# Third convolution tile's taps ahead of the split of the sums, and the residual added to h by VectorE late in the turn, in the state space stage of a four-stage language model kernel

## What is computed

```python
def _block(x, ...):                          # x: layernorm(h)
    h = _ln(x, ln1_w, ln1_b)
    zxbcdt = einsum('bld,pd->blp', h, in_proj_w)     # z | xBC | dt
    xBC = silu(sum(xp[:, k:k+L] * conv_w[:, k] for k in range(4)) + conv_b)
    dt = softplus(dt + dt_bias); dA = exp(dt * -exp(A_log))
    # recurrence over 512 steps: hn = hprev*dA + dt*x (outer) B ; y = hn . C
    y = (ys + D_skip * xs) * silu(z)
    y = y * rsqrt(mean(y*y) + EPS) * ssm_norm_w
    x = x + einsum('bli,di->bld', y, out_proj_w)     # called x2 in the kernel
    f = einsum('bld,hd->blh', _ln(x, ln2_w, ln2_b), fc1_w)
    f = f[..., :HIDDEN] * silu(f[..., HIDDEN:])
    return x + einsum('blh,dh->bld', f, fc2_w)
h = h + _block(_layernorm(h), ...)
```

## Time and profile before

| what | value |
|---|---|
| median of 3 runs | 2181.28 us (2177.38 to 2182.77) |
| the profiled execution | 2185.66 us |
| its span in the profile | 2183.2 us |
| state space stage | about 930 to 1398 us of the span |
| from the end of one turn to the end of the next, middle turns | 51.0 us |
| TensorE busy | 1947.5 us (89%) |
| VectorE busy | 1153.1 us (53%) |
| ScalarE busy | 743.0 us (34%) |
| GpSimd busy | 443.9 us (20%) |

### The profile page before, as it was taken

One profiled execution on the slowest core, in us unless ns is written; L12 is line 12 of the kernel. 1 busy time (PEld: TensorE's weight loads), 2 busy tenths in 40 slices (PEclk: granted clock), 3 DMA queues, 4 the chain that ended last, 5 costly groups with the idle time before them and its releaser, 6 DMA issues. The chain is left out here.

```text
span 2183.2 us, 27922 instructions
## 1 busy us (share of the span) xinstructions
PE 1947.5 (89%) x10040; PEld 1224.6 (56%) x10048; DVE 1153.1 (53%) x2695; ACT 743.0 (34%) x1249; POOL 443.9 (20%) x534
## 2 busy tenths in 40 slices
PE   4997618999999999758999998699999999999997
PEld 2343503344444444435556655465567888888886
DVE  5798577666666665246777776337412222222221
ACT  1434002554555545444555554121111111111111
POOL 5200200120122111111211111110371322322232
PEclk9988558999999999968999999789999999999999
DMA  2610002111112111000000000200123321222221
GB/s 64 226 39 0 0 18 80 51 58 52 53 36 63 51 53 32 1 31 6 6 6 6 6 6 6 98 1 1 52 75 93 69 58 33 64 61 60 67 36 19
DMA packets 68747, 94.72 MB, mean 43 GB/s; under 512 B 15387, under 2 KB 57663, under 8 KB 66338
## 3 DMA queue, kind: packets, MB, share of 16 engines
q1 hardware_dynamic: 52482, 77.19, 10.9%
q0 software_dynamic: 16128, 15.76, 4.1%
HBM read 54.96 MB, written 39.47 MB: 43 GB/s over the span
## 5 line engine op out<-in xcount | busy, mean ns | idle before, releaser
L972 DVE TENSOR_REDUCE row_max<-c_ps_m 128x1 f32<-128x512 f32 x384 | 252.7, 686 | 115.9 <-PE c_ps_m L1130 110.5
L1308 ACT ACTIVATE e<-c_ps_s 128x512 f32<-128x512 f32 x384 | 216.6, 596 | 222.1 <-PE c_ps_s L1146 221.3
L2596 DVE TENSOR_TENSOR e_f<-e_ps_u,e_gate 128x512 f32<-128x512 f32 x120 | 83.0, 691 | 271.6 <-ACT e_gate L2878 179.5
L2397 POOL DMA_INDIRECT out<-m_o,m_row_of x80 | 125.7, 1571 | 282.6 <-issue 262.2
L2813 PE MATMUL e_ps_o<-m_w,e_f 128*128 128x192 f32 x960 | 162.7, 327 | 0.9 <-DVE e_f L2596 0.9
L1130 PE MATMUL c_ps_m<-c_kT,qT 96*128 96x512 bf16 x384 | 150.4, 398 | 11.0 <-DVE row_max L972 10.9
L2813 PEld LDWEIGHTS e_ps_o<-m_w,e_f 128*128 128x128 f32 x960 | 158.1, 190 | 3.2 <-DVE e_f L2596 1.3
L1146 PE MATMUL c_ps_s<-qT,c_kT 97*128 97x512 bf16 x384 | 145.7, 390 | 12.2 <-ACT e L1308 5.0
L2878 ACT ACTIVATE e_gate<-e_ps_g 128x512 f32<-128x512 f32 x120 | 71.6, 597 | 242.3 <-PE e_ps_g L2787 162.3
L2781 PE MATMUL e_ps_g<-m_xT,m_w 128*128 128x256 f32 x480 | 129.7, 393 | 1.0 <-DVE h L2428 1.0
L2781 PE MATMUL e_ps_u<-m_xT,m_w 128*128 128x256 f32 x480 | 123.2, 379 | 0.0
(11 more groups left out here) (441 smaller groups left out, 3761.1 us busy)
## 6 DMA issues: line engine op xcount, KB each, us to landing
dealt<-x SPq DMA_DIRECT2D x8, 1290.0 KB, 15.1
m_x<-dealt SPq DMA_DIRECT2D x40, 258.0 KB, 2.7
spread<-parts SPq DMA_DIRECT2D x24, 384.0 KB, 2.4
qT<-spread SPq DMA_DIRECT2D x144, 64.0 KB, 2.3
c_kT<-spread SPq DMA_DIRECT2D x144, 64.0 KB, 2.4
m_w<-in_w13e SPq DMA_DIRECT2D x8, 1152.0 KB, 5.2
m_w<-in_w2e SPq DMA_DIRECT2D x8, 576.0 KB, 6.3
out<-h SPq DMA_DIRECT2D x8, 384.0 KB, 4.5
```

The lines of the kernel that those rows point to most:

```text
L972: dve.tensor_reduce(row_max[:, n // J, n % J:n % J + 1], ps_m[:, n % 2, :], AX_X, ALU.max)\
L1308: act.activation(e[:, n % LIVE_E, :], ps_s[:, n % 2, :], ACT.Exp, scale=QSCALE).then_inc(e_ready, 1)
L2397: pool.indirect_dma_start(out=out_rows, out_offset=bass.IndirectOffsetOnAxis(ap=row_of[:, n % 2, r:r + 1], axis=0), in_=o[:, n % 2, r, :], ...
L2596: dve.tensor_tensor(fe[:, n % 2, 2 * i:2 * i + 2, :], ps_ue[:, q % 2], gate_e[:, q % 2], ALU.mult)\
```

## The change

Two edits. In VectorE's turn, the taps of convolution tile 2 come ahead of `split_sums`, and those of tile 3 follow it directly; `mean_square`, which stood between the taps of tiles 2 and 3, now follows tile 3. And x2 is added to h by VectorE, as one `tensor_tensor` over 128x768 with a drain behind it, just ahead of `add_o`; GpSimd's add, the semaphore `x2_added` and both waits on it are gone.

```diff
@@ GpSimd, turn(t)
                     pool.wait_ge(v2_ready, t + 1)
                     pool.tensor_tensor(rstd2[:, :], var2[:, :], kit.minus_half[:, 0:J], ALU.pow).then_inc(r2_ready, 1)
-                    here = kit.h[:, t * J:(t + 1) * J, :]
-                    pool.tensor_tensor(here, here, x2[:, :, :], ALU.add).then_inc(x2_added, 1)
@@ VectorE, add_out(t, k)
                 if k == 0:
                     dve.wait_ge(rms_ready, t + 1)
-                    if t > 0:
-                        dve.wait_ge(x2_added, t)
@@ VectorE, new
+            def add_x2(t):
+                here = kit.h[:, t * J:(t + 1) * J, :]
+                dve.tensor_tensor(here, here, x2[:, :, :], ALU.add)
+
@@ VectorE, add_o(t, k)
                 dve.wait_ge(w_psum, place[key] + 1)
-                if k == 0:
-                    dve.wait_ge(x2_added, t + 1)
@@ VectorE, turn(t)
                 if begins:
+                    conv_tile(u, 2)
                     split_sums(u)
-                    conv_tile(u, 2)
+                    conv_tile(u, 3)
                 if ends:
                     mean_square(t)
-                if begins:
-                    conv_tile(u, 3)
                 if ends:
                     add_out(t, 0)
                     add_out(t, 1)
...
                     for j in range(J - 1):
                         times_c(u, j)
                 if ends:
+                    add_x2(t)
+                    dve.drain()
                     add_o(t, 0)
                     add_o(t, 1)
```

More of the change, by code:

```diff
@@ L1483, in state_space_block @@
          l_ready, log_ready, parts_ready, conv_ready, conv_done, spread_ready, mt_ready, rest_ready, state_ready,
-         yy_ready, totals_ready, decays_ready, ms_ready, rms_ready, v2_ready, r2_ready, y2_ready, x2_added) = kit.sems(
+         yy_ready, totals_ready, decays_ready, ms_ready, rms_ready, v2_ready, r2_ready, y2_ready) = kit.sems(
             "d_loaded d_made d_sel_ready d_tables d_a_exp d_w_scaled d_w_psum d_y_psum d_c_moved d_v1_ready d_r1_ready d_y_ready d_abs_ready "
             "d_e_ready d_u_ready d_l_ready d_log_ready d_parts_ready d_conv_ready d_conv_done d_spread_ready d_mt_ready "
-            "d_rest_ready d_state_ready d_yy_ready d_totals_ready d_decays_ready d_ms_ready d_rms_ready d_v2_ready d_r2_ready d_y2_ready d_x2_added")
+            "d_rest_ready d_state_ready d_yy_ready d_totals_ready d_decays_ready d_ms_ready d_rms_ready d_v2_ready d_r2_ready d_y2_ready")
         by_act = {k: kit.sem(f"d_{k}_by_act") for k in "y x z row ec cb bt sq y2 g".split()}
```

## The result

The changed kernel takes 2160.76 us (median of 4 runs, 2159.49 to 2161.76) against 2180.36 for the kernel before (median of 4). The ratio is 0.991, with a 95% interval of 0.9893 to 0.9928: 0.7 to 1.1% faster. The forecast was 2164.6 in a range of 2159 to 2173. A second pair of measurements, on a chip on which the kernel before took 2227 us, gave 0.9912 (0.9879 to 0.9945).

A forecast was written before the change was run, and what follows sets the result against it. TensorE was taken to set the pace, with waits on ScalarE and VectorE. Seven turns x 2.0 us, plus 1.5, plus 1.2, made 16.7 us off the median of 2181.3, forecasting 2164.6 us, 0.8% faster, range 2159 to 2173.

The forecast's parts named there:

- The bound and the two causes: Middle turn: TensorE sets the pace, idle 2.5 us; upstream, VectorE idles 1.81 before the split and loses 1.50 at a scaling.
- Taps first: VectorE, tile 2's taps before the split: the wait covers all but 0.51 us; tile 3's taps end 1.88 earlier.
- The root at 1.02: Mean square behind tile 3: the root takes 1.02 us instead of 1.44, so the output sum starts 0.57 earlier.
- The stalled scaling: Second norm's first scaling on VectorE stands until GpSimd's residual add ends; 1.50 us lost per turn.
- The rival that it comes from something that stays: First scaling's 1.87 us not caused by waiting for GpSimd's add; only 5.2 us gained, 2176.1 us; chance 0.08.
- Both chains allow 2.0: Second norm's rows on TensorE: the norm chain and the ScalarE and TensorE chain both allow a step 2.0 us earlier.
- The rival in which a turn gains only 1.5: Transposes come only 1.5 us earlier or the root keeps 1.44; 13.2 us gained in all, 2168.1 us; chance 0.16.
- The add at the seam: VectorE's residual add at the turn's end: about 0.95 us, covered by waits with some 0.7 of cover, costed at nothing.
- Turn -1: Start of the stage, without mean square: tile 3's taps end earlier and TensorE waits for ScalarE; 1.2 us gained.
- The last turn: End of the stage, without taps: gains the scalings' 1.50 us; the added add fits in a wait of 2.31.
- The sum: Whole kernel: 7 turns x 2.0, plus 1.5, plus 1.2, is 16.7 us; forecast 2164.6 us.
- The slower rival: Experts stage's first 102 us: TensorE's clock stays at 1.2 GHz, 34 us lost, 2199 us; chance 0.04.

The follow-up runs named there:

- experiment 11: Changed kernel with GpSimd's root for the first norm of sequence t + 2 behind all four dtx_rest products, not between second and third; 2152.48 us, 0.9864 of the kernel before.
- experiment 9: Changed kernel with the mean square ahead of the taps of tile 3 instead of behind them; 0.991 of the kernel before, turn 48.87 us.
- experiment 1: Kernel before with only VectorE's new order of taps, split and mean square; GpSimd keeps the residual add; 0.9962 of the kernel before, turn 50.60 us.
- experiment 2: Kernel before with only the residual add moved to VectorE at the turn's end, old order kept; 0.9968 of the kernel before, turn 50.58 us.
- experiment 4: Changed kernel with the residual add on GpSimd at the seam, behind the turn's last output add; 0.9935 of the kernel before, turn 49.81 us.
- experiment 7: Changed kernel with two more 128x768 adds on VectorE at the seam, a drain between; 0.9983 of the kernel before, mean turn 51.69 us.
- experiment 6: Changed kernel with one more 128x768 add on VectorE at the seam; 0.994 of the kernel before, turn 49.57 us.

## Why the prediction was right

*The bound and the two causes.* Right. TensorE's waits for ScalarE's exponentials (0.98), for the copy of cb (0.24) and for the second norm (0.46) are all gone, and the turn lies 2.06 us lower, at 48.93, for 49.0 foretold. Of the foreseen ceiling of 2.5 us the wait of 0.45 for the scaled rows remains. But the ceiling, read from TensorE's idle time, was none: the turn of experiment 11 is 50.99 - 48.38 = 2.61 us shorter than that before. The matmuls' busy time of one turn shrank with it, from 48.48 us before to 48.12 after and 47.83 in experiment 11, so some of the waiting stood inside the busy time.

*Taps first.* The split between the two groups of taps has no wait, as worked out. The 0.51 us on the mean square are there (the stretch to the mean square of turn 0 grew by 0.57) and cost nothing, as experiment 9 shows. The gain at the output sum was to be 0.57: from the mean square to the scalings pass 5.80 us instead of 6.82, less the 0.51, so it is 0.51.

*The root at 1.02.* Right, 1.01 in all turns, and shown: without taps beside it the root takes 1.01 (experiment 1 too), beside them 1.44 (experiments 2 and 9). By the Trainium skill's rule (SBUF — State Buffer, Who interferes with whom) a VectorE instruction with two SBUF inputs contends with a GpSimd instruction that reads SBUF, and the later one is blocked. That one is held agrees with the root, with the product beside GpSimd's (1.41 for 0.95) and with the 1.60 of experiment 4; but the root lost 0.43 us, and not the 0.58 to the tap's end that the prediction worked out from the rule, so the rows were the better guide.

*The stalled scaling.* Right, and shown: 1.87 with the add of 1.81, 1.52 with one of 1.47, 0.77 with a memset of 0.74, 0.38 with nothing. The rival that it comes from something that stays is out.

*Both chains allow 2.0.* This was the boldest step, since it rested on two estimates that came out equal. Experiments 1, 2 and 9 bear it out: 0.39 and 0.41 alone (0.6 and 0.7 at full clock), 2.06 together, and less than 0.1 for a norm chain that is earlier still. That two chains of estimates came out within 0.1 us of each other, and of the truth, is in part luck. The rival in which a turn gains only 1.5 is out.

*The add at the seam.* Costed at nothing with a cover of 0.7: measured, the wait for dt shrank by 0.26 and TensorE did not wait. The cover left beyond the add is 0.56 for the first bank and 0.36 for that of the second state, which the prediction names but works out no cover for.

*Turn -1.* The term was mis-sized: 1.2 foretold, 3.49 measured. The taps of tile 3 ended 13.96 us behind the turn's first tap instead of 15.11, 1.15 earlier, as worked out. What I had left out is TensorE's clock. Stretches before, then after; the clock is third from the end:

```profile
965.40:968.70 3.30, 0.00 (x0) 0.00 (x0) 0.10 (x1) 3.12 (x7) 0.00 (x0) 0.62 0.00 0
968.70:976.00 7.30, 7.23 (x39) 6.28 (x39) 1.44 (x3) 4.48 (x10) 0.89 (x2) 0.50 0.01 2
```

```profile
956.00:960.00 4.00, 3.96 (x23) 2.34 (x23) 2.04 (x3) 1.76 (x2) 0.00 (x0) 0.59 0.00 0
...
961.30:966.00 4.70, 4.28 (x39) 3.49 (x39) 1.05 (x3) 4.38 (x11) 0.34 (x1) 1.00 0.01 3
```

TensorE's wait for ScalarE's exponentials in this turn, before and after:

```profile
968.77 0.59 PE L1883 MATMUL d_ps_w<-after,ident 128*128 128x512 bf16 x1 [4.49 <-ACT seg L2098]
```

```profile
961.47 0.38 PE L1882 MATMUL d_ps_w<-after,ident 128*128 128x512 bf16 x1 [0.53 <-ACT seg L2097]
```

Before, TensorE waited 2.35 us for the parts, spread them at the full clock, stood still for 4.49 us until ScalarE's exponentials, and did the 39 matmuls of the next stretch at 1.2 GHz in 7.2 us. Now it waits 3.45 us ahead of the spreading, does most of that at the lower level, where ScalarE's table load and decays cover it, and the same 39 run at 2.4 GHz in 4.3. All ten profiles of kernels with the new order have 35.9 to 36.9 us here, all three with the old one 40.4.

*The last turn.* Mis-sized the other way, and it hides the first: 1.5 foretold, 0.12 measured in the stretch from the mean square to the end. The scalings did gain 1.47. But the 24 matmuls of the output projection took 4.82 us instead of 4.42, and behind TensorE's pause, shorter now by 1.5 us, the clock came back later: from the first of the second norm's rows to the last projection into h pass 14.84 us instead of 13.91. The projections at 1358 to 1363 ran at 0.51 of full clock, where before it was 0.70 at 1383 to 1388:

```profile
1358.00:1363.00 5.00, 5.00 (x8) 1.17 (x4) 0.00 (x0) 0.60 (x1) 0.00 (x0) 0.51 0.00 0
```

```profile
1383.00:1388.00 5.00, 5.00 (x12) 1.52 (x10) 0.69 (x1) 0.60 (x1) 0.00 (x0) 0.70 0.00 0
```

This stretch varies from 28.1 to 31.3 us over the profiles, among them 31.25 in experiment 1, where its instructions are those of the kernel before. So the same instructions can take 2 us more or less here, with the clock. Since the two profiles of each kernel agree (29.19 and 29.14, 29.07 and 28.80), whether the lost 1.4 us belong to the change is not shown.

*The sum.* Foretold by the same landmarks: -1.2, +0.5, -12.0, -2.5, -1.5, together -16.7. Measured: -3.5, +0.6, -12.4, -2.5, -0.1, together -17.9. The runs' 19.6 is 1.7 more, within the interval of 15.7 to 23.3.

*The slower rival.* The first 102 us of the experts stage had a granted clock of 0.85 after 0.83, so nothing was lost there:

```profile
1373.00:1475.00 102.00, 89.88 (x374) 55.83 (x374) 49.43 (x188) 24.10 (x41) 11.64 (x68) 0.85 0.13 53
```

The sum of this rival was wrong, though. At 0.83 the 102 us hold 84.7 us of work at full clock; at 0.50 these take 169 us, so where TensorE sets the pace 67 us would be lost and not 34, and the kernel would be slower than before by 0.3% from a clock of about 84.7 / 125.2 = 0.68 on, not 0.60.

Left open: why the clock returns sooner in one execution of the last turn than in another, and why it falls in some turns of experiments 1, 2 and 7 and not in others that have the same waits.

## What to carry to other kernels

When two chains meet at one instruction, measure an edit on one of them together with an edit on the other: here each alone was worth 0.4 us per turn in the mean (0.6 to 0.7 at full clock) and both 2.06, and either might have been dropped as not worth keeping. Look at the turns one by one before averaging them: one turn at low clock among six took over a third of each edit's gain out of the mean. Look in the trace for a first instruction of a group that is much longer than its median; if it ends with an instruction of GpSimd, move that one away, and choose the new place by what VectorE runs there. An add moved to VectorE is free only as long as the wait that covers it lasts, and past that it can cost more than its own length, since TensorE's clock may fall behind the new wait.

## What the runs showed of the hardware

- A GpSimd instruction holds a VectorE scaling of 128x192 in SBUF that starts just behind it until it has ended, even if it only writes: the longest of four scalings was 1.87, 1.52 and 0.77 us beside instructions of 1.81, 1.47 and 0.74, and the other three stayed near 0.37. In all 24 cases of the three kernels the scaling started 0.06 to 0.09 us behind GpSimd's instruction and ended 0.11 to 0.12 us behind its end. The Trainium skill (SBUF — State Buffer, Who interferes with whom) has such full blocking for VectorE's two-port modes, which it says a `tensor_scalar` can enter. The rows agree with the blocking; in which mode the scaling ran no run shows.
- A wait of TensorE of 1.34 us in the middle of busy turns was followed by a granted clock of 0.57 over 4 us in one turn, by 0.50 over some 10 us in another, and by no fall in four of six. In experiment 1 it was 0.50 over some 3 us behind a wait of 1.40 in one turn of six, and stayed at full speed behind waits of 1.30 to 1.36 in the others. In experiment 2 it was 0.51 over some 3 us in one of six turns that all have a wait of 0.98. With a wait of 0.31 at the seam (experiment 6) no turn was more than 0.1 us longer than the others. The kernel before has the wait of 0.98 too, and its six turns took 50.98 to 51.00.
- In turn -1, having the low-clock stretch at another place was worth more (3.49 - 1.15 = 2.3 us) than the reordered work itself (1.15).
